# Factors of the second layer made in the last chunk of the first, and a table of slots dealt anew

## The reference, cut to what matters

```python
xn = (xs - mu) * lax.rsqrt(var + 1e-05) * ln_w + ln_b      # layer 0: over channels
xb, z = split(einsum('blc,dc->bld', xn, in_proj_w), 2)     # 768 + 768 channels
xc = silu(conv(xb) + conv_b)
dt, Bm, Cm = split(einsum('bld,ed->ble', xc, x_proj_w))    # 24 + 16 + 16
dt = softplus(dt @ dt_w.T + dt_b)
h = exp(dt * A) * h + dt * x * B                           # scan over 4096 tokens, 16 states
y = (h @ C + xc * D) * silu(z)
x = x + y @ out_proj_w.T
qkv = gn(x) @ qkv_w.T                                      # layer 1: attention in windows of 64 tokens
x = x + softmax(q @ k.T * scale) @ v @ proj_w.T + proj_b
```

## Time and profile before

| | |
|---|---|
| median of 3 runs | 6579.67 us (6577.32 to 6579.70) |
| the profiled execution, its own time | 6579.83 us |
| its span in the trace | 6577.7 us |
| busy: PE, DVE, ACT, POOL | 92%, 90%, 76%, 78% of the span |
| start of chunk 0, chunk 1, chunk 31 (first scan of each) | 123.41, 294.1, 5200.3 us |
| last output of the scan layer's DVE | 5367.7 us |
| `group_affine` on DVE | 5371.53 to 5377.4 us |
| first projection of the attention | 5387.78 us |

### The profile page before, as it was taken

The page is one execution under the profiler, slowest core; times in us unless marked ns, Lnnn a source line. Parts: engine busy times, 40 slices in busy tenths (PEclk is TensorE's granted clock), DMA queues, the critical chain, the costliest instruction groups (busy, mean ns, idle before and its releaser), DMA issues. The chain is left out here.

```text
span 6577.7 us, 105792 instructions
## 1 busy us (share of the span) xinstructions
PE 6067.4 (92%) x35452; PEld 3884.7 (59%) x35452; DVE 5924.9 (90%) x7357; ACT 5010.0 (76%) x10458; POOL 5105.1 (78%) x4137
## 2 busy tenths in 40 slices
PE   7999999999999999999999999999999869999998
PEld 3555555555555555555555555555555557777776
DVE  6999999999999999999999999999999976666666
ACT  3888888888888888888888888888888854343443
POOL 2999999999999999999999999999999961010100
PEclk8999999999999999999999999999999989999999
DMA  6222222222222222222222222222222312222222
GB/s 262 102 100 100 100 100 100 100 100 100 100 101 100 101 100 100 100 100 102 102 101 100 100 100 100 100 100 100 100 100 100 119 43 71 84 84 81 91 74 72
DMA packets 175235, 656.80 MB, mean 100 GB/s; under 512 B 28044, under 2 KB 28268, under 8 KB 149860
## 3 DMA queue, kind: packets, MB, share of 16 engines
q1 hardware_dynamic: 174692, 650.05, 26.9%
...
## 5 line engine op out<-in xcount | busy, mean ns | idle before, releaser
L967 POOL TENSOR_TENSOR dbx<-u,bb 128x512 f32<-128x512 f32 x3072 | 3836.1, 1276 | 261.5 <-DVE h L811 210.4
L801 DVE TENSOR_TENSOR_SCAN p_da<-p_da,state_v,dbx 128x512 f32<-128x512 f32 x1728 | 2165.3, 1274 | 0.8 <-ACT p_da L627 0.6
L627 ACT ACTIVATE p_da<-dt,neg_a 128x512 f32<-128x512 f32 x3072 | 2091.0, 692 | 72.5 <-DVE h L811 27.0
L811 DVE TENSOR_TENSOR_SCAN h<-p_da,state_h,dbx 128x512 f32<-128x512 f32 x1344 | 1703.8, 1275 | 138.1 <-ACT p_da L627 106.4
L1108 PEld LDWEIGHTS p_yt<-ident,hc_v 128*128 128x128 f32 x6912 | 872.0, 146 | 803.4 <-issue 644.8
L820 DVE TENSOR_TENSOR hc_v<-cc,p_da 128x512 f32<-128x512 f32 x1728 | 1144.5, 672 | 24.0 <-PE p_yt L1108 20.4
L1037 PE MATMUL p_g<-xs,win 128*128 128x512 f32 x2304 | 1155.6, 599 | 3.8 <-DVE xs L770 3.4
L1108 PE MATMUL p_yt<-ident,hc_v 128*128 128x128 f32 x6912 | 1074.7, 283 | 87.0 <-DVE hc_v L820 85.4
L976 POOL TENSOR_TENSOR hc_g<-h,cc 128x512 f32<-128x512 f32 x768 | 978.2, 1274 | 0.0
L1033 PE MATMUL p_g<-xb,cdiag 128*128 128x512 f32 x1536 | 766.0, 595 | 1.9 <-ACT halo L573 1.9
L661 ACT ACTIVATE hct<-p_yt,ct 128x128 f32<-128x128 f32 x2304 | 655.7, 373 | 44.5 <-PE p_yt L1147 44.5
...
## 6 DMA issues: line engine op xcount, KB each, us to landing
bb<-bc_spill SPq DMA_DIRECT2D x128, 1024.0 KB, 10.1
...
```

The lines of the kernel that those rows point to most:

```text
L627: nc.scalar.activation(p_da[n % RD][:], dt[:, d % 2, :], ACT.Exp, scale=neg_a[:, d, n:n + 1])\
L801: nc.vector.tensor_tensor_scan(psum, psum, dbx[:, n % RB, :], state_v[:, d, k:k + 1], ALU.mult, ALU.add).then_inc(s_scan, 1)
L811: nc.vector.tensor_tensor_scan(h[:, k, :], psum, dbx[:, n % RB, :], state_h[:, d, k:k + 1], ALU.mult, ALU.add).then_inc(s_scan, 1)
L967: nc.gpsimd.tensor_tensor(dbx[:, n % RB, :], u[:, d % 2, :], bb[:, n, :], ALU.mult)\
```

## The change

1. `group_affine` goes. The images 0 to 2 get their factors of layer 1 in the last chunk, as part 2 of the `affine` functions, in the slots in which chunk 0 makes those of the images 1 to 3. Image 3's are made inside the attention: two small matmuls on PE behind the third and the sixth projection, the small DVE and ACT steps around them.
2. The first scaling of the attention (`scale(0, 0)`) is made by ACT in slot 65 of the last chunk (`scale_first`); the attention's ACT starts with a table preload instead.
3. Slots are dealt anew, in all chunks: the tables below.

```diff
-TURN_STATE_AT, TIMES_CT_AT, KEEP_AT = (8, 9, 13), (8, 12, 14), 13
-LAG, LAG_V, LAG_G = 4, 2, 6
+TURN_STATE_AT, TIMES_CT_AT, KEEP_AT = (8, 10, 13), (8, 12, 14), 13
+LAG, LAG_V, LAG_G = 3, 2, 5
-MEAN_AT, CENTRE_AT, SQUARE_AT = 4, (4, 7, 10), (3, 7, 9)
+MEAN_AT, CENTRE_AT, SQUARE_AT = 0, (3, 7, 10), (3, 7, 8)
-OUT_AT, OUT_SLOTS, RESIDUAL_AT = (7, 12, 18), (4, 4, 3), (11, 17, 24)
+OUT_AT, OUT_SLOTS, RESIDUAL_AT = (7, 12, 18), (3, 3, 1), (13, 17, 22)
-... COPY_CT_AT, SCALE_AT = ... 86, (88, 89, 93)
+... COPY_CT_AT, SCALE_AT = ... 91, (86, 89, 94)
-DT_AT, SOFTPLUS_AT, DT_X_AT = 6, 6, 12
+DT_AT, SOFTPLUS_AT, DT_X_AT = 6, 6, 14
...
-        group_affine(nc, "mid", stats, quarter, eps_col, gsc, gbi)
-        attention_layer(nc, x1_d, out, ident, gsc, gbi, space)
+        attention_layer(nc, x1_d, out, ident, gsc, gbi, space, stats, quarter, eps_col)
...
+        AFFINE = ((0, 1, 0), (1, NBATCH, AFFINE_STEPS), (0, NBATCH - 1, AFFINE_STEPS + NBATCH + 6))
...
+            def scale_first():
+
+                act.wait_ge(s_afd, AFFINE[2][2] + NBATCH + 6)
+                for j in range(NJ):
+                    nc.scalar.activation(space["x0"][:, j, :], space["x0"][:, j, :], ACT.Identity, scale=gsc[:, 0:1],
+                                         bias=gbi[:, 0:1]).then_inc(s_x0, 1)
...
-                        if i == 0 and d * NS + n == AFFINE_AT[3]:
-                            affine(1)
+                        if i in (0, NCH - 1) and d * NS + n == AFFINE_AT[3]:
+                            affine(1 if i == 0 else 2)
...
+            act.sem_inc(s_xn, NJ)
+            act.preload_act_table_set(EXP_LN)
...
-            scale(0, 0)
             high_weights("wq")
...
+                if k == NQ - 1:
+                    pe.wait_ge(s_gd, 2)
+                    nc.tensor.matmul(g_m, quarter[:], g_mean[:], start=True, stop=True).then_inc(s_gm, 1)
+            pe.wait_ge(s_gd, 5)
+            nc.tensor.matmul(g_v, quarter[:], g_sq[:], start=True, stop=True).then_inc(s_gm, 1)
             values(0, 0, 0)
```

More of the change, by code:

```diff
@@ L668, in affine @@
                 act.wait_ge(s_afm, 2 * part + 2)
-                images = slice(0, 1) if part == 0 else slice(1, NBATCH)
+                images = slice(*AFFINE[part][:2])
                 nc.scalar.activation(af_rs[:, images], af_v[:, images], ACT.Ln, bias=eps_col[:, 0:1]).then_inc(s_afa, 1)
@@ L745, in _ @@
             copy_y(NCH, 0)
+            act.wait_ge(s_x0, NJ)
         @block.vector
@@ L835, in affine_means @@
             def affine_means(part):
-                first, last = (0, 1) if part == 0 else (1, NBATCH)
-                dve.wait_ge(s_sd, last * CPB * NJ)
+                first, last, done = AFFINE[part]
+                if part < 2:
+                    dve.wait_ge(s_sd, last * CPB * NJ)
+                else:
+                    dve.wait_ge(s_stat, (last * CPB + 1) * NJ)
                 for b in range(first, last):
@@ L841, in affine_means @@
                     nc.vector.bn_aggr(af_mv[:, b, :], stats[:, at:at + per]).then_inc(s_afd, 1)
-                done = part * AFFINE_STEPS + last - first
-                dve.wait_ge(s_afd, done)
+                dve.wait_ge(s_afd, done + last - first)
                 nc.vector.tensor_copy(af_mean[:, first:last], af_mv[:, first:last, 0]).then_inc(s_afd, 1)
             def affine_variance(part):
-                at = slice(0, 1) if part == 0 else slice(1, NBATCH)
-                done = part * AFFINE_STEPS + (2 if part == 0 else NBATCH)
+                first, last, done = AFFINE[part]
+                at, done = slice(first, last), done + last - first + 1
                 dve.wait_ge(s_afm, 2 * part + 1)
@@ L856, in affine_result @@
             def affine_result(part):
-                first, last = (0, 1) if part == 0 else (1, NBATCH)
-                at = slice(first, last)
-                done = part * AFFINE_STEPS + (5 if part == 0 else NBATCH + 3)
+                first, last, done = AFFINE[part]
+                at, done = slice(first, last), done + last - first + 4
+                if part == 2:
+                    dve.wait_ge(s_lna, NCH * 8)
                 dve.wait_ge(s_afa, 2 * part + 2)
@@ L1152, in affine @@
             def affine(part):
-                at = slice(0, 1) if part == 0 else slice(1, NBATCH)
-                first = part * AFFINE_STEPS + (2 if part == 0 else NBATCH)
+                first, last, done = AFFINE[part]
+                at, first = slice(first, last), done + last - first + 1
+                if part == 2:
+                    pe.wait_ge(s_ct, NCH)
                 pe.wait_ge(s_afd, first)
@@ L1196, in body @@
                                     out_step(i, j, t)
-                        if i == 0 and g == AFFINE_AT[1]:
-                            affine(1)
+                        if i in (0, NCH - 1) and g == AFFINE_AT[1]:
+                            affine(1 if i == 0 else 2)
                         if q == NCH and d > 0 and n in LAST_OUT_AT:
@@ L1235, in _, with attention_layer @@
                 last_out_step(2, t)
-def attention_layer(nc, x1, out, ident, gsc, gbi, space):
+def attention_layer(nc, x1, out, ident, gsc, gbi, space, stats, quarter, eps_col):
     with ExitStack() as ctx:
@@ L1277, in attention_layer @@
         p_d = [bank("p_d0"), bank("p_d1")]
+        g_mv, g_mean, g_dev, g_sq, g_rs, g_bi = (sb(f"g_{v}", [P, c]) for v, c in (
+            ("mv", 2), ("mean", 1), ("dev", 1), ("sq", 1), ("rs", 1), ("bi", 1)))
+        g_m, g_v = p_o[0][:, 0:1], p_o[0][:, 1:2]
+        s_gd = sem("a_affine_dve")
+        s_gm = sem("a_affine_mm")
+        s_ga = sem("a_affine_act")
         s_zero = sem("a_zeroed")
@@ L1431, in _ @@
             copy_v(0, 0)
+            act.wait_ge(s_gm, 2)
+            nc.scalar.activation(g_rs[:], g_v, ACT.Ln, bias=eps_col[:, 0:1]).then_inc(s_ga, 1)
+            act.wait_ge(s_ga, 1)
+            nc.scalar.activation(g_rs[:], g_rs[:], ACT.Exp, scale=-0.5).then_inc(s_ga, 1)
             def body(g, r):
@@ L1524, in _ @@
             upper_bits(1, 1)
+            last_image_means()
+            last_image_variance()
             copy_v(0, 0)
+            last_image_result()
             def body(g, r):
```

92 lines of the change are left out of this document (34 added, 58 removed).

## The result

The changed kernel takes 6523.57 us (median of 4 runs, 6519.90 to 6528.43), the kernel before, run beside it, 6578.49 (4 runs, 6576.80 to 6579.70). The ratio is 0.9916, with an interval of 0.9904 to 0.9928: 55 us, or 0.8%. The profiled execution takes 6525.62 us with a span of 6523.8, so the two traces lie 53.9 us apart in span.

The account below looks back on a forecast made before the run. The prediction took DVE to set the pace (157.46 of 162.07 us a chunk), so only its waits could be won; the terms summed to -73.1 us, giving 6506.7 us, with an 8-in-10 range of 6482 to 6560.

Parts of the forecast that it names:

- The product buffer of d = 5: DVE's 0.66 us wait for PE: ACT's 0.59 us wait ends, so 0.55 of it goes in each chunk, -17 us.
- The decays of d = 4: DVE's wait for ACT at state 5: PE's filled gap shortens ACT's waits, 2.30 us becomes 1.5, -24.5 us.
- the add of state 6: In d = 3, now ahead of the input step ACT waits for: that step comes 0.43 us earlier.
- The lag of POOL's products: POOL's products one slot earlier with dt_x in slot 14: POOL does the same work, taken at 0.
- the mean's move: Mean in slot 0, centre in slot 3: PE runs it where it would idle, DVE's wait goes, -27.1 us.
- R3: Rival: POOL becomes the bound because its 24 products a chunk may wait for their scans, 6650 us; chance 0.13.
- The low clock behind the moved gap: PE's idle time ahead of the gate lowers its clock; DVE waits 0.61 us for the Exp in 25 chunks, +15.
- The gate's wait: Wait of 0.38 us in each of 31 chunks: PE gets its gap back in d = 1, -11.8 us.
- The last chunk: DVE makes the factors of three images there: +4.9 us; ACT's three scalings in slot 65 hidden.
- The Exp of the factors: In the last chunk, a wait of 0.50 us within the +4.9, read from chunk 0.
- the first projection's delay: Between the layers, DVE's memset starts at 5372.1 instead of 5378.61: -6.5 us, a delay of 9.8 instead of 16.3.
- The attention: PE gets two small matmul pairs inside its bound stretch, about 0.55 us each: +1.1.

Follow-up runs that it names:

- Number 7: The changed kernel with the last step of the x projection in slot 82 for 81 and ACT's copy of it in 83: 6517.67 us.
- number 3: The changed kernel with transposed state 7 back in slot 9 instead of 10: 6554.79 us.
- number 5: The changed kernel with POOL's own products one slot later again (LAG 4, LAG_G 6) and dt x back in slot 12: 6549.42 us.
- number 4: The changed kernel with the mean and the first centre back in slot 4: 6524.73 us.
- 9: The changed kernel with five more matmuls that nobody reads, one in slot 3 and four in slot 5, in chunks 1 to 30: 6516.47 us.

## Why the prediction was right, and where its steps were not

The sum was -73 us and came to -54: the way and the range were right, the mechanism in part. Three steps were wrong in a way that the sum shows, and a fourth, the gate's, went the right way for a reason that is not known.

**The product buffer of d = 5 is the step that failed.** "[...] with `silu` and PE that much earlier most of the 0.66 goes; I take 0.55: -17." It is -1.8. The step took ACT's 0.59 us wait for PE as the cause. It did go, but ACT then stood 0.27 us for DVE instead: it was at its full lead, and `silu` could come no sooner against DVE. Number 7 shows the rest: with the buffer freed in time 0.53 us come as a decay wait. The bound of the term, 0 "if ACT finds another wait", was the right end.

**The decays of d = 4 were right**, mechanism and size (1.5 predicted, 1.45 found), and number 3 shows the cause. One part of the explanation did not show: the add of state 6 was to take 0.43 us back from the step that ACT waits for. Both of ACT's waits went whole (0.52 + 0.36 = 0.88; the wait of d = 4 fell by 0.86), and with the adds back (number 5) it stays at 1.45.

**The lag of POOL's products, taken at 0, is the second.** I looked at POOL, which indeed cost nothing (its idle time is 6.2 us a chunk against 6.7). The edit is worth 26 us through PE, at a place the prediction did not look at: the add of state 0, whose move ahead of the gate the change had shown. It shortens PE's idle time there from 2.29 to 1.85 us, and with that the low level comes in 18 chunks and not in 27. That this gain, which no term had, came together with the mean's move, whose low clock it made rarer, is luck. R3 falls too: DVE's list has no wait for a late `dbx`.

**The low clock behind the moved gap is the third.** The prediction saw it and priced it at the Exp alone, in 25 chunks: it was 18, +10.6. But ACT's decays stand behind the same steps: where the level is low throughout, the four output steps that now lie ahead of transposed state 4 make them late, +10.5. Together 21 us of waits, against 15. The table of the result and the numbers 4 and 9 show that cause. The Trainium skill (TensorE: Matmul & The Clock Gate, "A second HAM failure mode: psum-queue depth-cycling") says that short idle times between groups of matmuls, repeated in each iteration, keep the clock going between its two levels. The trace agrees. Read as a cost in every chunk, as the prediction read it, it does not hold: the Exp's wait is in 18, and in the 16th chunk the clock stays at 1.00. The moved low clock also explains what I had least expected: that the mean's move, the largest term, is worth nothing by itself (number 4). The row of -27.1 in the table of terms is a wait that went, not time won.

**The gate's wait fell, but not by the step given.** The prediction took it from PE's filled gap, which comes back "in the same way" in d = 1. With that gap open again (number 3) the gate's wait does not come back, so its cause is open and its direction was luck.

**Small sizes.** At the gate 0.14 us are left of 0.38. The last chunk costs 7.4 and not 4.9. DVE is busy 5.2 us longer there, and one small copy of the factors, in none of the prediction's terms, takes 1.70 of them (in chunk 0 the same copy takes 0.17 us; why is open):

```profile
5150.96 1.70 DVE L802 COPY af_mean<-af_mv 128x3 f32<-128x3 f32 x1
```

The Exp of the factors costs 0.87 where the sum had 0.50, and the 0.81 at the gate was not in the sum. The prediction counted the first projection's delay from the start of the factors at 5371.53 (16.3 us). From the scan layer's last output it was 20.1 us and is 13.6: shorter by 6.4, as forecast. The attention gained 2.2 where I had +1.1: the matmul pair at 5343.96 takes 0.28 us and not 0.55, and the granted clock of the first 40 us from the first projection is 0.96 instead of 0.88, in this one pair of executions (columns as in the earlier trace rows, after and then before); why is open.

```profile
5336.12:5376.12 40.00, 37.08 (x338) 30.87 (x339) 18.66 (x45) 14.46 (x30) 4.00 (x3) 0.96 0.13 38
```

```profile
5387.78:5427.78 40.00, 36.88 (x292) 30.29 (x293) 15.89 (x34) 12.75 (x25) 3.99 (x3) 0.88 0.13 36
```

The 2.1 us at the starts of three images (`state_v`, 6.4 against 4.3) are not explained either.
